# Keys and values of an attention layer from two TensorE products a part of x in place of three

## The reference, cut to what matters

```python
x = hidden_states                                 # 4 x 512 x 1024, fp32
n = layernorm(x)
q  = (n @ Wq)                                     # 1024 -> 32 heads of 32
kv = n @ Wkv                                      # 1024 -> 64: 32 of keys, 32 of values, shared by all heads
scores = q @ k.T * 32**-0.5 + alibi, causal       # per head, 512 x 512
x = x + softmax(scores) @ v @ Wo
x = x + layernorm(x) @ dequantized(qweight).T + bias
```

## Time and profile before

| | before |
|---|---|
| times of 3 runs | 866.9, 862.15, 860.96 us (median 862.15) |
| the profiled execution | 856.82 us, of it a span of 855.1 us |
| PE busy | 831.9 us (97% of the span) |
| DVE busy | 543.8 us (64%) |
| ACT busy | 361.5 us (42%) |
| POOL busy | 391.1 us (46%) |
| PE clock granted, mean | 0.994 of full speed |

### The profile page before, as it was taken

The page is one execution under the profiler, slowest core; times in us unless marked ns, Lnnn a source line. Parts: engine busy times, 40 slices in busy tenths (PEclk is TensorE's granted clock), DMA queues, the critical chain, the costliest instruction groups (busy, mean ns, idle before and its releaser), DMA issues.

```text
span 855.1 us, 13739 instructions
## 1 busy us (share of the span) xinstructions
PE 831.9 (97%) x4732; PEld 602.6 (70%) x4732; DVE 543.8 (64%) x1526; ACT 361.5 (42%) x701; POOL 391.1 (46%) x254
## 2 busy tenths in 40 slices
PE   5999899999999999999999999999999999999998
PEld 3887688888756555555656554688888888888886
DVE  5866373546767788887887784465555555554545
ACT  3655446212356776677666666322111221111211
POOL 0000000000078888888888889584333344444211
PEclk9999999999999999999999999999999999999999
DMA  9666866485445656455656663845443333334211
GB/s 334 261 204 221 291 197 216 150 191 173 123 117 141 148 143 142 127 167 141 145 138 173 163 151 89 216 105 150 126 117 100 100 98 111 99 99 123 75 50 49
DMA packets 87565, 127.41 MB, mean 149 GB/s; under 512 B 8788, under 2 KB 42612, under 8 KB 87416
## 3 DMA queue, kind: packets, MB, share of 16 engines
q1 hardware_dynamic: 87344, 126.27, 52.0%
q10 hardware_dynamic: 152, 0.27, 0.1%
HBM read 87.17 MB, written 38.94 MB: 147 GB/s over the span
## 4 chain that ended last, share of the span: by engine, by line
PE 88%; ACT 3%; DMA 3%; issue 2%; DVE 2%; SPq 1%; POOL 1%; DVEq 0%; ACTq 0%
PE p_st L797 13%; PE p_o L779 11%; PE p_s L779 10%; PE p_st L711 10%; PE p_o L722 9%; PE p_o L617 9%; PE p_s L684 9%; PE p_s L617 7%; PE p_o L735 4%; PE p_st L617 2%; DMA ql_d<-ql 1%; ACT junk L850 1%; PE p_s L797 1%; PE p_st L701 1%; PE p_st L811 1%
## 5 line engine op out<-in xcount | busy, mean ns | idle before, releaser
L1128 DVE CUSTOM_DVE_ANT_0 spill<-p_s,mask 128x128 bf16<-128x128 f32 (+3 forms) x512 | 223.6, 482 | 61.3 <-PE p_s L684 59.1
L918 ACT ACTIVATE pt<-p_st 128x512 f32<-128x512 f32 (+1 forms) x352 | 178.3, 559 | 88.5 <-PE p_st L711 88.0
L518 POOL TENSOR_SCALAR_AFFINE_SELECT pt<-pt 128x512 f32<-128x512 f32 x128 | 83.0, 662 | 271.8 <-ACT pt L918 271.8
L684 PE MATMUL p_s<-kst,xt 98*128 98x128 f32 (+3 forms) x512 | 149.7, 331 | 1.8 <-DMA xt<-ext_d 1.5
L711 PE MATMUL p_st<-xt,kst 100*128 100x512 f32 (+1 forms) x352 | 141.5, 406 | 2.4 <-ACT pt L918 1.5
L525 POOL TENSOR_TENSOR pt<-pt 128x1536 f32<-128x1536 f32 x32 | 111.7, 3490 | 2.7
L684 PEld LDWEIGHTS p_s<-kst,xt 98*128 98x128 f32 x512 | 98.8, 194 | 15.0 <-DVE mx L1128 2.3
L617 PE MATMUL p_o<-xt,wqh 128*128 128x512 f32 x272 | 96.3, 401 | 0.0
L541 POOL TENSOR_TENSOR osl<-ob,osh 128x1024 fp32r<-128x1024 f32 x14 | 33.7, 2407 | 133.8 <-ACT osh L954 133.7
L711 PEld LDWEIGHTS p_st<-xt,kst 100*128 100x128 f32 x352 | 66.7, 190 | 39.1 <-DVE ml L1135 18.7
L722 PE MATMUL p_o<-pt,vst 128*32 128x512 f32 (+3 forms) x1024 | 89.8, 445 | 0.0
(11 more groups left out here) (134 smaller groups left out, 1344.7 us busy)
## 6 DMA issues: line engine op xcount, KB each, us to landing
xt<-qh_d SPq DMA_DIRECT2D x64, 256.0 KB
xs<-in_x_t_dram SPq DMA_DIRECT2D x32, 256.0 KB, 5.6
qh_d<-qh SPq DMA_DIRECT2D x32, 256.0 KB, 2.6
ql_d<-ql SPq DMA_DIRECT2D x32, 256.0 KB, 3.2
xt<-ql_d SPq DMA_DIRECT2D x32, 256.0 KB
o_d<-o_st SPq DMA_DIRECT2D x32, 256.0 KB, 2.7
ob<-o_d SPq DMA_DIRECT2D x64, 128.0 KB, 4.0
inv_b<-inv_d SPq DMA_DIRECT2D x64, 128.0 KB, 4.5
```

Source lines behind the costliest of these rows:

```text
L518: pool.affine_select(out=own, in_=own, compare_op=ALU.is_ge, fill=0.0, base=0, pattern=[[0, 4], [1, P]], channel_multiplier=-1).then_inc(c ...
L684: pe.matmul(scores_of(n), qst[s % 4][0:R_MAX, j, qb * P:(qb + 1) * P], kst[0:R_MAX, b * S:b * S + keys], start=True, stop=True).then_inc(s ...
L918: act.activation(pt[s % 2][:, j:j + heads, PT_AT[kb]:PT_AT[kb] + KB_LEN[kb]], p_st[:, place(k) % 3, 0:heads * KB_LEN[kb]].rearrange("p (j ...
L1128: dve.tensor_tensor_reduce(spill[:, SPILL_AT[qb]:SPILL_AT[qb] + keys], scores_of(n), mask[:, S - keys:S], 1.0, LOWEST, ALU.add, ALU.max, m ...
```

## The change

The weights of the keys and values lie side by side in one tile wkv2: columns 0 to 63 the high parts (keys, values), columns 64 to 127 the low parts. For a part c of x, one matmul of all 128 columns with x's high part gives high x high in PSUM rows 0 to 63 and low x high in rows 64 to 127; a second one of 64 columns adds high x low to rows 0 to 63. The two halves are then added: ACT copies rows 64 to 127 to a tile kv in SBUF (`low_weights`), DVE adds rows 0 to 63 to it, and writes the keys' three copies and the values from there with four instructions of 32 rows.

```diff
-            wkvh, wkvl = sb("wkvh", [P, CK, P], F32R), sb("wkvl", [P, CK, P], F32R)
+            wkv2 = sb("wkv2", [P, CK, P], F32R)
+            kv = sb("kv", [64, S])
@@ TensorE, keys_values(b, c)
-                last = chunk(p_kv, wkvh, wkvl, slice(0, P), b, c)
+                pe.matmul(p_kv, wkv2[:, c, :], xt(b, 0)[:, c, :], start=(c == 0), stop=False, skip_group_check=True)
+                last = pe.matmul(p_kv[0:64, :], wkv2[:, c, 0:64], xt(b, 1)[:, c, :], start=False, stop=(c == CK - 1),
+                                 skip_group_check=True)
@@ ScalarE
+            def low_weights(b):
+                act.wait_ge(kv_done, b + 1)
+                at_least(act, kt_done, 4 * b)
+                act.copy(kv[:, :], p_kv[64:P, :]).then_inc(kv_low, 1)
+
             def project(b):
                 more = b < LASTB
                 if 0 < b < LASTB:
                     for t in range(TPB):
                         statistics(4 * b + 4 + t)
+                low_weights(b)
                 for m in range(CK):
...
-            for g in range(4):
-                src = raw_kv[:, :, 0:32] if g < 3 else raw_kv[:, :, 32:64]
-                act.copy(wkvh[:, :, 32 * g:32 * g + 32], src).then_inc(kv_hi, 1)
+            act.copy(wkv2[:, :, 0:64], raw_kv[:, :, :]).then_inc(kv_hi, 1)
@@ VectorE, keys_values(b)
-                dve.wait_ge(kv_done, b + 1)
+                dve.wait_ge(kv_low, b + 1)
+                dve.tensor_tensor(kv[:, :], kv[:, :], p_kv[0:64, :], ALU.add).then_inc(kv_sum, 1)
...
-                dve.scalar_tensor_tensor(out=kt[0:96, :], in0=p_kv[0:96, :], scalar=SCALE, in1=rstd_b[0:96, b % 2, :],
-                                         op0=ALU.mult, op1=ALU.mult).then_inc(kt_done, 1)
-                dve.tensor_tensor(kt[96:P, :], p_kv[96:P, :], rstd_b[96:P, b % 2, :], ALU.mult).then_inc(kt_done, 1)
-                dve.wait_ge(kt_done, 2 * b + 1)
+                dve.wait_ge(kv_sum, b + 1)
+                for r in (0, 32, 64):
+                    dve.scalar_tensor_tensor(out=kt[r:r + 32, :], in0=kv[0:32, :], scalar=SCALE, in1=rstd_b[0:32, b % 2, :],
+                                             op0=ALU.mult, op1=ALU.mult).then_inc(kt_done, 1)
+                dve.tensor_tensor(kt[96:P, :], kv[32:64, :], rstd_b[32:64, b % 2, :], ALU.mult).then_inc(kt_done, 1)
+                dve.wait_ge(kt_done, 4 * b + 3)
...
-            for g in range(4):
-                src = raw_kv[:, :, 0:32] if g < 3 else raw_kv[:, :, 32:64]
-                dve.wait_ge(kv_hi, g + 1)
-                dve.tensor_tensor(wkvl[:, :, 32 * g:32 * g + 32], src, wkvh[:, :, 32 * g:32 * g + 32], ALU.subtract).then_inc(kv_lo, 1)
+            dve.wait_ge(kv_hi, 1)
+            dve.tensor_tensor(wkv2[:, :, 64:P], raw_kv[:, :, :], wkv2[:, :, 0:64], ALU.subtract).then_inc(kv_lo, 1)
```

More of the change, by code:

```diff
@@ L184, in layer @@
         pair_done = sem("pair_done")
-        kv_in, kv_hi, kv_lo = sem("kv_in"), sem("kv_hi"), sem("kv_lo")
+        kv_in, kv_hi, kv_lo, kv_low, kv_sum = (sem(n) for n in ("kv_in", "kv_hi", "kv_lo", "kv_low", "kv_sum"))
         wq_hi, wq_lo = sem("wq_hi"), sem("wq_lo")
@@ L320, in spread_stats @@
                 at_least(sp, q_freed, CK * (b - 1))
-                at_least(sp, kt_done, 2 * (b - 1))
+                at_least(sp, kt_done, 4 * (b - 1))
                 sp.dma_start(rstd_b[:, b % 2, :], st_d[b:b + 1, S:2 * S].to_broadcast([P, S])).then_inc(rstd_in, 16)
@@ L621, in keys_values @@
                 if c == 0:
-                    pe.wait_ge(kv_lo, 4)
-                    at_least(pe, kt_done, 2 * b)
+                    pe.wait_ge(kv_lo, 1)
+                    at_least(pe, kv_sum, b)
                 pe.wait_ge(x_lo, CK * b + c + 1)
-                last = chunk(p_kv, wkvh, wkvl, slice(0, P), b, c)
+                pe.matmul(p_kv, wkv2[:, c, :], xt(b, 0)[:, c, :], start=(c == 0), stop=False, skip_group_check=True)
+                last = pe.matmul(p_kv[0:64, :], wkv2[:, c, 0:64], xt(b, 1)[:, c, :], start=False, stop=(c == CK - 1),
+                                 skip_group_check=True)
                 if c == CK - 1:
@@ L639, in turn_v @@
             def turn_v(b):
-                pe.wait_ge(kt_done, 2 * b + 2)
+                pe.wait_ge(kt_done, 4 * b + 4)
                 at_least(pe, vst_done, b)
```

## The result

| | before | with the change |
|---|---|---|
| median of 4 runs | 861.56 us (860.34 to 866.9) | 874.44 us (871.74 to 877.39) |
| profiled execution | 856.82 us, span 855.1 | 874.76 us, span 873.0 |
| ratio of the runs | | 1.0153, 95% interval 1.0107 to 1.020 |

The account below looks back on a forecast made before the run. PE was taken as the bound, busy 97% of the span. Batches 0 and 1 cost 10.8 us, batch 2 4.2, batch 3 gains 0.4: +14.6 on the median 862.15 gives 876.8, forecast 877 us, range 868 to 884.

Parts of the forecast that it names:

- three places: PE takes from DVE: batch 0's bank for query group 5, statistics turns of batches 1 and 2; slack 2.0, 0, near 0.
- All three waits: PE idles 5.4 us at batch 0's bank, waits some 10 at batch 1's statistics turn and 4.0 at batch 2's.
- The saving: PE's keys and values: one of three matmuls a part goes, 0.18 us saved a part, 1.4 a batch, 5.8 in all.
- DVE's chain: DVE from the sum to the first qt of a batch: 4.5 us (4.2 to 4.8), before 2.6.
- 0.4 us was to be kept: Batch 3: PE waits 0.8 us for group 1's bank and keeps about 0.4 of its 1.4 saved.
- the 1.0: Batch 0: ACT's statistics come 1.0 us earlier because PE saves 6 x 0.18 ahead of them; copy starts at 48.7.
- Rival 3: Keys and values on PE: the narrow matmul costs what the removed one did; +16.8 us, 879 us; chance 12%.
- Rival 2: Batch 0: ACT's waits for ql stores to land swallow the 4.9 us delay; +9.6 us, 872 us; chance 12%.
- The cold clock: After long waits in batches 0 and 2, PE's clock falls to near half; 24 matmuls take 1.6 us more.

Follow-up runs that it names:

- The gate alone: Kernel before, with an idle 64x512 copy on ACT behind its statistics, for which DVE waits instead of for PE; ratio 1.0128.
- The third matmul again: Changed kernel with each part's first matmul made twice, second timing, beside a rerun of the changed kernel; ratio 1.0226, median 878.37 us.
- the copy early: Changed kernel with ACT's copy moved ahead of some or all of its statistics in batches 0 to 2; ratio 1.0020.
- Six products: Changed kernel with DVE's three products of 32 rows made twice; ratio 1.0342, median 888.47 us.
- the third matmul: Changed kernel with each part's first matmul made twice, timed on two occasions; ratios 1.0232 and 1.0226 to the kernel before.
- the second: The changed kernel, unaltered, timed and profiled once more against the kernel before; ratio 1.0204, median 877.54 us.
- matmuls alone: Kernel before with the change's two matmuls a part and weights, halves not added, DVE as before; ratio 0.9961.
- copy on DVE: Changed kernel with the low half's copy made by DVE in front of the sum instead of by ACT; ratio 1.0007.

## Why the prediction was right

- **Which stretch, which wait.** It was forecast that PE has slack 2.0, 0 and near 0 us at three places, and that the copy stands behind ACT's statistics. All three waits came: 5.73 at 54.87 (5.4 at 54.55), 4.90 + 4.38 up to 105.96 (some 10 up to 105.1), 4.42 at 160.01 (4.0 at 158.9, 148.1 + 10.8). The first of the two in batch 1 stands at the turn of the values, which waits for kt and which the forecast had not named. The runs split the cost, by their last queries. The gate alone adds 9.75 us. The third matmul again differs from it in little but DVE's longer chain and adds 18.74, so the chain behind the gate costs 9.0, four times its growth of 2.24. The saving gives back 2.3. With the copy early, the same chain and the saving together leave only 2.4: the queue on ACT is what makes the chain cost its full length.
- **DVE's chain** was 4.84 us for the 4.5 taken, just above the 4.2 to 4.8. The mis-sized terms are the pitch of the three products and the sum's hand-over. I took the products at 0.60 twice, as a like pair of 128 rows; they run 0.71 apart (2.11 for three), and 0.82 stand between the sum's start and the first product. Two chains at 0.34 too little are 0.7 of the 0.9 us by which the turn in batch 1 came later than forecast (105.96 for 105.1), three are 1.0 of the 1.1 in batch 2 (160.01 for 158.9). Six products confirm that an added microsecond here counts about four times, five where the clock joins in.
- **The saving** was taken as 1.4 us a batch; the narrow matmul costs 0.23, not 0.28, so it was 1.8. It made no difference: in batch 3, where 0.4 us was to be kept, nothing was. Before batch 3 the changed kernel is 188.97 - 172.84 = 16.1 us late, at the last query 16.1. The saving counts in full there, as the third matmul shows, but the longer path to the first qt costs as much: 0.97 us are the bank's wait; where the other 0.8 go no run separates, and some 0.3 of it stands ahead of a score at 215.17 that waits for DVE's maxima.
- **Luck in batch 0.** It was taken that ACT's statistics come 1.0 us earlier there, because PE saves six times 0.18 ahead of them. They do in this pair: ACT's copy starts at 48.66, forecast 48.7. But with three matmuls a part it starts at 49.08 (gate alone), 48.89 and 49.97 (third matmul), with two at 48.66 and 49.14. The two profiles differ by as much as the term is worth, and in the changed one PE loses 1.14 and 0.65 us to waits for x in this pass. The hit is luck in part; the 1.0 is not shown.
- **The rule on tiling modes.** Rival 3 was wrong: 128, 64 and 128 columns follow each other at 0.23 us as equal ones do. By the statement in the Trainium skill ("TensorEngine Tiling (Array Packing)", Key Properties) that a change of tiling mode drains the engine, each pair would have cost more, if going from 128 to 64 columns is such a change. This trace shows no drain there, and it does not say which mode a matmul ran in. What makes the 0.26 and 0.28 in attention is open: those matmuls also differ in their type and in their waits.
- **Rival 2** fell too: ACT's two waits for stores of ql were 2.97 and 3.63 us, the same as the 3.05 and 3.58 before, 5 us later. The transfers moved with their issues.
- **The cold clock** was priced at 1.6 us a wait from the earlier trace rows. Batch 2 paid it: from the turn to batch 3 it is 28.96 us, before 27.37. The granted clock behind the three waits was near a half, as forecast (PE's windows: stretch, length, busy and count, granted clock, DMA share, GB/s):

```profile
54.00:58.00 4.00, 3.13 (x7) 0.50 0.40 131
...
106.00:110.00 4.00, 4.00 (x12) 0.59 0.57 194
...
160.00:164.00 4.00, 3.99 (x12) 0.57 0.58 199
```

- **The total.** Forecast +14.6; the projection grew by 16.1 in the profile and 16.5 in the second (some 0.7 more each, for the late start of before's profile), the runs by 12.9 and by 18.5 us (medians; 1.53 and 2.04% by the ratios). The forecast lies between the two occasions; the sign and the mechanism are shown, the last 2 us of the size are not. That 877 lies 2.6 us from the 874.44 measured is partly luck: the same +14.6 on the second occasion's 859.0 gives 873.6, 3.9 below its 877.54.

## What to carry to other kernels

An engine that is idle half of the time can still be the wrong place for a new step: look at what stands ahead of the step in that engine's written order at the moment its input is ready, not at the engine's share. When the bound engine runs without waits, ask at each hand-over how much earlier than needed the other side is; here it was 2.0, 0 and 0 us, and a delay was paid once in each batch while the saving was not. The same reading gives the cure: work that frees a bank or feeds a turn goes first in its engine's order, which alone was worth 0.55%.

## What the runs showed of the hardware

**When TensorE's clock falls.** Twenty-four matmuls behind a wait take 5.44 to 5.49 us at the full level and some 7 where it has fallen. After waits of 2.97 us (before, batch 1), 3.63 (matmuls alone), 3.66 (copy on DVE), 4.42 (the change, batch 2) and 4.68 (copy early) they took 6.94 to 7.11 (elsewhere, behind 4.38 to 4.84 us, between 6.66 and 7.74); after 2.60 us (copy early, batch 2), 2.71 (copy on DVE, batch 2) and 0.58 (gate alone, batch 2) 5.47 to 5.49. The chain of the early copy shows one of each:

```profile
95.91 7.11 PE p_o L619 x24
...
148.20 5.47 PE p_s L619 x24
```

So the wait of 4.68 us cost 1.6 more than itself and that of 2.60 nothing more. The length of the wait does not decide alone: with the third matmul the wait in batch 2 was 2.62 us in both its profiles, and the 24 matmuls behind it took 7.08 and 7.11. What else decides is open.

**Pitch on VectorE.** Products of 32 rows to different rows of one tile start 0.71 us apart though none waits for another; like instructions of 128 rows start 0.60 apart. Which of the differences between the two pairs counts, the number of rows or the row at which they start, these do not tell; but the qt of 128 rows, too, starts 0.71 behind the instruction on rows 64 to 95 in front of it (53.41 to 54.12). Rows made no such instruction shorter: 0.68 us at 32, 64, 96 and 128 rows of 512 columns.
